# A decoder layer on one core: where the expert matmuls of the cross phase stand in the slots, and a gate of sixteen columns

## The chip, the cores and the metric

One core of one Trainium2 chip. The metric is the device time of one execution in microseconds, the median of three runs.

## What is computed

Eight sequences of 512 tokens and 512 features pass one decoder layer with a LayerNorm behind each of its three parts: a self-attention with a second, causal linear term; a cross-attention of 16 heads over a context of the same shape; and a feed-forward of two experts with a gate. Only the last part and the output projection of the second are touched. Cut to what matters:

```python
x = layernorm(x + xattn(ctx, ctx, x, Wv, Wk, Wq, Wo, bo))      # ends in  out @ Wo.T + bo
logits = x @ gate_w                                            # [4096, 512] @ [512, 8]
topk_w, topk_idx = top_k(softmax(logits), 2)
e0, e1 = silu(x @ w0 + b0), silu(x @ w1 + b1)                   # each [4096, 512] @ [512, 512]
out = e0 * topk_w[0] * (topk_idx[0] == 0) + e1 * topk_w[1] * (topk_idx[1] == 1)
x = layernorm(x + out)
```

Everything is float32 to the outside. Large products are made of a high and a low part of each operand (`F32R` tiles), as high times high, low times high and high times low: three matmuls for one.

## The kernel before, in words

The program has three phases, written out by hand for each engine: self-attention, the memory term with its projection, and the cross phase, which this change is about. It fills the time from about 861 us to the end.

**Slots.** The cross phase goes through 512 slots, `n` = 0 to 511. A slot is one key tile of one head: 16 slots make a group of four heads, 64 slots a batch (one sequence). In each slot PE makes two matmuls of 512 columns: the transposed scores (L1576), of which ACT takes the exponential into `cpt` (L1839), and the scores of a slot 22 later (L1547), of which DVE takes the row maximum (L1557). PE may be two slots ahead of either: the scores of slot n wait for the exponential of slot n-2, and L1547 of slot n for the maximum of slot n-2. In each group, at its slot 9 and at slot 4 of the next, PE multiplies two key tiles by the values (L1618), and at slot 4 of the next it adds up the exponentials (L1654), of which POOL has by then added three tiles into `cross_added` (L2094, at slots 7, 11 and 15 of each group). DVE takes the reciprocals of the sums at slots 5 to 8 (L1929).

**Work behind.** Beside batch B's slots run the output projection, LayerNorm, gate, experts and last LayerNorm of batch B-1, at slots given by tables at L1477 to L1503. A slot number over 63 lies in the next batch. Each engine works through its own program in slot order, and within a slot in the order of `cross_slot_tensor` and its siblings. The steps:

- `PROJECT`: output projection, tile k of 128 tokens times chunk c of 512 features, three matmuls for each pair (L1722 to L1724), with one matmul for the bias ahead of c = 0 (L1668). `ADD`, `FACTORS`, `APPLY`: residual and second LayerNorm (DVE, POOL, ACT).
- `TRANSPOSE`: four transposes on PE of a finished tile (L1702). One slot later ACT copies the high part, and at `LOW` DVE makes the low part (L2355). Tiles k = 0, 2 use bank 6, and 1, 3 bank 7.
- `GATE`: four slots of three matmuls each (L203 to L205 in `triple`), with 8 stationary columns. `LOGITS`: four transposes to tokens by experts (L1714). DVE and ACT then make the two weights of each token in bank 7.
- `EXPERT`: eight units (4 tiles, 2 experts), each of 12 matmuls of 512 columns (L1749), three slots a unit, four matmuls a slot, from slot 44 to 67. Units 0 and 1 have their bias from PE, the others from ACT, which writes it to the bank ahead (`cross_bias_written`, L1891 to L1894).
- For each unit then: tanh on ACT (L1870) one slot after its last matmul, silu on DVE (L1975) one slot later, the gate's weight on ACT (L1875) one later, and the add to the tile on POOL (L2064) one later. Tanh of unit u waits for POOL's add of unit u-2, since there are two `tanh` tiles.
- `STATS3`, `FACTORS3`, `APPLY3`, `STORE`: the third LayerNorm and the output of each tile.

The last batch has nothing to hide behind and is done in a tail, which keeps its order of work.

## Time and profile before

| | us |
|---|---|
| median of 3 runs | 1716.77 |
| lowest, highest | 1716.08, 1717.36 |
| the profiled execution | 1717.48 |
| its span, first to last instruction | 1714.9 |
| granted clock of PE, mean | 0.988 of full speed |
| cross phase, first exponential to the last one of slot 511 | 861.1 to 1653.2 |
| one batch of 64 slots, undisturbed | 101.85 |

The span is 2.6 us shorter than the execution's own time. Between 1000 and 1600 us the granted clock is 1.00. The batches there repeat to within a few hundredths of a microsecond, so that one of them stands for six. The rows below are of the batch whose slot 0 has its exponential at 1255.0 us, and of the start of the next one, whose slot 0 has it at 1356.9.

### The profile page before, as it was taken

Reading aid. Unit: us, or ns where it says so; the run is one execution under the profiler, and the core shown is the slowest. Engines: PE = TensorE matmul, PEld = TensorE weight load, DVE = VectorE, ACT = ScalarE, POOL = GpSimd, SP = SyncE. Lnnn points to the kernel's source line nnn. Section 1 sums busy time; section 2 is a strip of 40 time slices with the busy share of each in tenths; the row PEclk is TensorE's granted clock in tenths of the full one; section 3 lists DMA queues with packets and bytes.
Section 4 is the critical chain, followed back from the end, with each engine's and each line's share of the span. In section 5 each row is a group of like instructions: output and inputs, shape, how many; then the busy total and the mean of one; then the engine's idle time right before and its main releaser. Section 6 shows DMA issues by size and latency. Waiting matters only on the chain.

```text
span 1714.9 us, 30931 instructions
## 1 busy us (share of the span) xinstructions
PE 1643.5 (96%) x10596; PEld 1118.3 (65%) x10596; DVE 1254.9 (73%) x2790; ACT 1004.7 (59%) x2010; POOL 1169.0 (68%) x967
## 2 busy tenths in 40 slices
PE   8999999999999889999998999999999999999998
PEld 5777777777777468877853556575565656656566
DVE  6777777777777567777876677868777687777745
ACT  4666666666665543333355566676666766666664
POOL 3566665666656555654467787878798787978874
PEclk8999999999999899999999999999999999999999
DMA  7665656656665455667436434525434443533210
GB/s 217 161 168 158 171 159 164 165 162 163 165 156 154 146 183 173 189 190 215 154 110 162 126 103 118 136 63 155 111 107 115 108 138 80 160 100 106 63 50 25
DMA packets 173463, 237.80 MB, mean 139 GB/s; under 512 B 22774, under 2 KB 76278, under 8 KB 173308
## 3 DMA queue, kind: packets, MB, share of 16 engines
q1 hardware_dynamic: 173308, 235.84, 49.9%
q8 instruction: 85, 1.39, 0.3%
q14 instruction: 70, 0.57, 0.1%
HBM read 92.10 MB, written 41.94 MB: 78 GB/s over the span
## 4 chain that ended last, share of the span: by engine, by line
PE 77%; POOL 10%; DVE 4%; issue 3%; DMA 3%; ACT 2%; SPq 1%; POOLq 0%; DVEq 0%; ACTq 0%
PE bank L1749 9%; PE bank L203 7%; POOL cross_added L2094 7%; PE bank L204 7%; PE bank L205 7%; PE bank L349 6%; PE bank L1576 5%; PE bank L1618 5%; PE bank L1547 5%; PE bank L403 5%; PE bank L416 4%; PE bank L1654 2%; PE bank L980 1%; PE bank L374 1%; PE bank L1006 1%
## 5 line engine op out<-in xcount | busy, mean ns | idle before, releaser
L1557 DVE TENSOR_REDUCE cross_negmax<-bank 128x1 f32<-128x512 f32 x512 | 337.7, 673 | 99.8 <-PE bank L1547 96.7
L1839 ACT ACTIVATE cpt<-bank 128x512 f32<-128x512 f32 x512 | 297.2, 593 | 139.0 <-PE bank L1576 115.6
L494 ACT ACTIVATE pt<-bank 128x256 f32<-128x256 f32 (+3 forms) x512 | 222.2, 437 | 209.2 <-PE bank L349 193.5
L2094 POOL TENSOR_TENSOR cross_added<-cross_added,cpt 128x2048 f32<-128x2048 f32 x61 | 280.1, 4591 | 14.0 <-ACT cpt L1839 13.4
L607 DVE CUSTOM_DVE_ANT_0 bank<-bank,future 128x128 f32<-128x128 f32 (+3 forms) x512 | 240.1, 489 | 64.0 <-PE bank L403 63.9
L1576 PE MATMUL bank<-cqk 98*128 98x512 f32 x512 | 224.8, 439 | 10.7 <-ACT cpt L1839 7.3
L1547 PE MATMUL bank<-cqk 96*128 96x512 f32 x512 | 215.1, 424 | 13.9 <-DVE cross_negmax L1557 11.0
L678 POOL TENSOR_SCALAR_AFFINE_SELECT pt<-pt 128x512 f32<-128x512 f32 x128 | 81.6, 638 | 214.0 <-ACT pt L494 213.9
L2094 POOL TENSOR_TENSOR cross_added<-cpt,cpt 128x2048 f32<-128x2048 f32 x32 | 146.6, 4582 | 83.7 <-ACT cpt L1839 83.7
L349 PE MATMUL bank<-qk 98*128 98x256 f32 (+2 forms) x512 | 180.2, 355 | 6.7 <-ACT pt L494 4.5
L403 PE MATMUL bank<-qk 96*128 96x256 f32 (+2 forms) x512 | 167.9, 329 | 3.9 <-DVE self_negmax L607 2.3
L1929 DVE RECIPROCAL bank<-bank 128x128 f32<-128x128 f32 x128 | 121.8, 954 | 67.2 <-PE bank L1654 67.2
L203 PE MATMUL bank<-xt_hi,w_hi 128*128 128x512 f32 x384 | 158.2, 412 | 2.5 <-DVE w_lo L566 1.9
L1576 PEld LDWEIGHTS bank<-cqk 98*128 98x128 f32 x512 | 97.0, 189 | 93.6 <-issue 39.9
L204 PE MATMUL bank<-xt_hi,w_lo 128*128 128x512 f32 x384 | 154.1, 401 | 0.0
L205 PE MATMUL bank<-xt_lo,w_hi 128*128 128x512 f32 x384 | 152.3, 397 | 0.0
L349 PEld LDWEIGHTS bank<-qk 98*128 98x128 f32 x512 | 96.3, 189 | 82.2 <-ACT pt L494 40.7
L644 DVE RECIPROCAL bank<-bank 128x128 f32<-128x128 f32 x128 | 121.9, 958 | 33.8 <-PE bank L374 33.8
L1547 PEld LDWEIGHTS bank<-cqk 96*128 96x128 f32 x512 | 95.9, 189 | 61.2 <-DVE cross_negmax L1557 39.2
L1618 PE MATMUL bank<-cpt,cv 128*32 128x512 f32 x1024 | 124.2, 603 | 0.0
L694 POOL TENSOR_TENSOR self_added<-self_added,pt 128x1024 f32<-128x1024 f32 x64 | 118.0, 1843 | 5.4
L694 POOL TENSOR_TENSOR self_added<-pt,pt 128x1536 f32<-128x1536 f32 x32 | 111.3, 3479 | 2.7
(213 smaller groups left out, 3622.4 us busy)
## 6 DMA issues: line engine op xcount, KB each, us to landing
qk<-stage SPq DMA_DIRECT2D x384, 128.0 KB, 2.4
cqk<-cstage SPq DMA_DIRECT2D x384, 128.0 KB, 2.4
scratch_memory<-memory SPq DMA_DIRECT2D x64, 256.0 KB, 3.7
ma<-scratch_memory SPq DMA_DIRECT2D x32, 512.0 KB, 4.0
raw<-in_x_t SPq DMA_DIRECT2D x32, 256.0 KB, 2.8
v<-in_x SPq DMA_DIRECT2D x32, 256.0 KB, 3.2
scratch_y_ar<-y_ar SPq DMA_DIRECT2D x32, 256.0 KB, 2.2
my_ar<-scratch_y_ar SPq DMA_DIRECT2D x32, 256.0 KB, 4.6
```

The source lines that it names most:

```text
L203: pe.matmul(out, a[0], b[0], start=first, stop=False)
L204: pe.matmul(out, a[1], b[0], start=False, stop=False)
L205: return pe.matmul(out, a[0], b[1], start=False, stop=last)
L349: pe.matmul(bank[:, 0:SEQ - q0], kq[0:98, 1, j, first:first + P], kq[0:98, 0, j, q0:SEQ], start=True, stop=True).then_inc(s.pe_st, 1)
L403: pe.matmul(bank[:, 0:max(keys, 256)], kq[0:96, 0, j, tile_of(qt)], kq[0:96, 1, j, 0:max(keys, 256)], start=True, stop=True).then_inc(s.pe ...
L607: dve.tensor_tensor_reduce(out=scores, in0=scores, in1=sh.future[:, SEQ - P * (qt + 1):SEQ], scale=-1.0, scalar=-NEG, op0=ALU.add, op1=ALU ...
L694: pool.tensor_tensor(out, old, pt[:, :, 0:SEQ - first], ALU.add).then_inc(s.pool_add, 1)
L1547: pe.matmul(max_bank(sh, m)[:, :], kq[0:96, 0, jm, tile_of(qt)], kq[0:96, 1, jm, :], start=True, stop=True).then_inc(s.pe_mx, 1)
L1557: dve.reduce_max(s.negmax[gm % 2][:, col:col + 1], max_bank(sh, m)[:, :], AX, negate=True).then_inc(s.dve_max, 1)
L1576: pe.matmul(sh.bank[2 + n % 2][:, :], kq[0:98, 1, j, tile_of(kt)], kq[0:98, 0, j, :], start=True, stop=True).then_inc(s.pe_st, 1)
L1839: act.activation(s.pt[step % 3][:, j, :], sh.bank[2 + n % 2][:, :], ACT.Exp, scale=SCALE_CROSS).then_inc(s.act_exp, 1)
L2094: pool.tensor_tensor(s.added[:, :, :], old[:, :, :], s.pt[step % 3][:, :, :], ALU.add).then_inc(s.pool_add, 1)
```

## The change

The tables move, and some of what they need is rewritten:

- The expert units start at slots 30, 41, 47, 51, 54, 58, 61 and 64, and take 6, 6, 4, 3, 4, 3, 3 and 3 slots. In slots 30 to 35 and 41 to 46 there are two expert matmuls a slot, in 47 to 50 and 54 to 57 three, in the rest four. They end at slot 66. Tanh, silu, weight and add follow by tables of their own.
- Unit 0 waits for tile 0's low part alone, and unit 1 for nothing of the gate. Of the biases, PE makes those of units 0 and 2, and ACT the six others.
- The banks: unit 0, 1 and all odd ones in bank 6, units 2, 4 and 6 in bank 7. Transposes of tiles 1 to 3 share bank 7, so that those of tiles 2 and 3 wait for the low part of the tile just before (slots 30 and 33, on DVE). `TRANSPOSE` and `LOW` of tile 3 come one slot later.
- The gate's high and low parts stand side by side as 16 stationary columns: two matmuls a chunk for three. The sum of both halves is made where the logits are turned: four float32 matmuls by a 16 x 8 matrix of ones take the place of the four transposes. ACT copies 16 rows for 8. The low weights now also meet the low activations, a term that was left out before.
- The projection's first six pairs stand at slots 5 to 10 for 4 to 9. The third LayerNorm's steps come up to three slots earlier.

```diff
-PROJECT = {4: (0, 0), 5: (0, 1), 6: (0, 2), 7: (1, 0), 8: (1, 1), 9: (1, 2), 15: (0, 3), 16: (1, 3), 17: (2, 0),
+PROJECT = {5: (0, 0), 6: (0, 1), 7: (0, 2), 8: (1, 0), 9: (1, 1), 10: (1, 2), 15: (0, 3), 16: (1, 3), 17: (2, 0),
...
-LOW = (29, 30, 33, 35)
-GATE, LOGITS, EXPERT = 37, 42, 44
+LOW = (29, 30, 33, 36)
+GATE, LOGITS = 37, 42
...
-STATS3, FACTORS3, APPLY3, STORE = (58, 64, 68, 76), (59, 65, 69, 78), (66, 71, 73, 81), (67, 72, 74, 82)
+STATS3, FACTORS3, APPLY3, STORE = (55, 62, 67, 75), (56, 63, 68, 77), (63, 70, 72, 80), (64, 71, 73, 81)
+UNIT = (30, 41, 47, 51, 54, 58, 61, 64)
+UNIT_SLOTS = (6, 6, 4, 3, 4, 3, 3, 3)
+PREFILL = {1: 39, 3: 50, 4: 53, 5: 57, 6: 60, 7: 63}
+TANH = (36, 47, 51, 54, 58, 61, 64, 67)
+SILU = (37, 48, 52, 55, 59, 62, 65, 68)
+WEIGH = (46, 49, 53, 56, 60, 63, 66, 69)
+JOIN = (47, 50, 54, 57, 61, 64, 67, 70)
...
-                    pe.wait_ge(s.dve_u, UNITS * b - 1 + k)
+                    pe.wait_ge(s.dve_u, UNITS * b - k)
...
-            pe.wait_ge(s.dve_x2t, TILES * b + k - 1)
+            pe.wait_ge(s.dve_x2t, TILES * b + k)
...
-        done = triple(pe, sh.bank[6][0:EXPERTS, :], (cw.gate_hi[:, c, :], cw.gate_lo[:, c, :]),
-                      (s.x2t_hi[:, c, :], s.x2t_lo[:, c, :]), c == 0, c == GROUPS - 1)
+        parts = sh.bank[7][0:2 * EXPERTS, :]
+        pe.matmul(parts, cw.gate[:, c, :], s.x2t_hi[:, c, :], start=(c == 0), stop=False)
+        done = pe.matmul(parts, cw.gate[:, c, :], s.x2t_lo[:, c, :], start=False, stop=(c == GROUPS - 1))
...
-            done = pe.transpose(sh.bank[7][:, k * EXPERTS:(k + 1) * EXPERTS], s.x1t[0:EXPERTS, tile_of(k)],
-                                sh.ident[0:EXPERTS, 0:EXPERTS])
+            done = pe.matmul(sh.bank[7][:, k * EXPERTS:(k + 1) * EXPERTS], s.x1t[0:2 * EXPERTS, tile_of(k)],
+                             cw.gate_sum[:, :], start=True, stop=True)
...
+        if u == 0:
+            pe.wait_ge(s.dve_x2t, TILES * b + 1)
+        elif u == 2:
+            pe.wait_ge(s.dve_gate, GATE_OPS * (b + 1))
+        else:
+            pe.wait_ge(s.act_bias, bias_written(b, u))
...
+    piece, pieces = 2 * at + half, 2 * UNIT_SLOTS[u]
+    for part in range(3 * GROUPS * piece // pieces, 3 * GROUPS * (piece + 1) // pieces):
```

How the built programs stand, in three places. In the rows L1576 and L1547 before are L1595 and L1566 after; L1749 is L1770, L1702 is L1721, L2094 is L2116, L2064 is L2086.

PE, slots 32 to 34, before:

```order
L1576 MATMUL bank<-cqk_131 128x512
L1547 MATMUL bank<-cqk_132 128x512
L1632 MATMUL bank<-x1t,a 128x512
L1576 MATMUL bank<-cqk_131 128x512
L1702 MATMUL bank<-ident,x_183 128x128 x4
L1547 MATMUL bank<-cqk_132 128x512
L1576 MATMUL bank<-cqk_131 128x512
L1547 MATMUL bank<-cqk_132 128x512
```

and now:

```order
L1595 MATMUL bank<-cqk_131 128x512
L1770 MATMUL bank<-exp_hi,x2t_lo 128x512
L1566 MATMUL bank<-cqk_132 128x512
L1651 MATMUL bank<-x1t,a 128x512
L1770 MATMUL bank<-exp_lo,x2t_hi 128x512
L1595 MATMUL bank<-cqk_131 128x512
L1770 MATMUL bank<-exp_hi,x2t_hi 128x512
L1566 MATMUL bank<-cqk_132 128x512
L1770 MATMUL bank<-exp_hi,x2t_lo 128x512
L1595 MATMUL bank<-cqk_131 128x512
```

Two matmuls of unit 0 stand in each slot, one ahead of the scores for the maximum and one behind; before, these slots had none.

PE, slot 4 (the matmuls by the values and the sums of a batch's last group stand here), before:

```order
L1576 MATMUL bank<-cqk_132 128x512
L1668 MATMUL bank<-bias_rows,bias_pick 128x512
L1722 MATMUL bank<-wo_hi,cy_hi 128x512
L1723 MATMUL bank<-wo_lo,cy_hi 128x512
L1724 MATMUL bank<-wo_hi,cy_lo_137 128x512
L1547 MATMUL bank<-cqk_133 128x512
L1618 MATMUL bank<-cpt_176,cv_178 32x512 x4
L1618 MATMUL bank<-cpt_174,cv_178 32x512 x4
L1654 MATMUL bank<-cross_added,ones 32x512 x4
```

and now, with the start of slot 5:

```order
L1595 MATMUL bank<-cqk_132 128x512
L1566 MATMUL bank<-cqk_133 128x512
L1637 MATMUL bank<-cpt_176,cv_178 32x512 x4
L1637 MATMUL bank<-cpt_174,cv_178 32x512 x4
L1673 MATMUL bank<-cross_added,ones 32x512 x4
L1595 MATMUL bank<-cqk_132 128x512
L1687 MATMUL bank<-bias_rows,bias_pick 128x512
L1742 MATMUL bank<-wo_hi,cy_hi 128x512
L1743 MATMUL bank<-wo_lo,cy_hi 128x512
L1744 MATMUL bank<-wo_hi,cy_lo_137 128x512
```

The projection's bias and first three matmuls have gone to slot 5, and slot 4 has only its own two and the group's work.

POOL, behind its add of slot 55 to that of slot 63 and one further (a row of `x` is the add of a unit to its tile, four rows from L187 to L193 a LayerNorm's factors), before:

```order
L2064 TENSOR_TENSOR x_183<-x_183,tanh_161 128x512
L2064 TENSOR_TENSOR x_183<-x_183,tanh_162 128x512
L187 TENSOR_SCALAR ln_rstd<-ln_mv 128x1
L189 TENSOR_TENSOR ln_rstd<-ln_rstd,ln_power 128x1
L191 TENSOR_TENSOR ln_shift<-ln_mv,ln_rstd 128x1
L193 TENSOR_SCALAR ln_shift<-ln_shift 128x1
L2094 TENSOR_TENSOR cross_added<-cross_added,cpt_176 128x2048
L2064 TENSOR_TENSOR x_183<-x_183,tanh_161 128x512
L2046 TENSOR_TENSOR cstage<-keys,cstage 128x512
L2094 TENSOR_TENSOR cross_added<-cross_added,cpt_174 128x2048
L2064 TENSOR_TENSOR x_183<-x_183,tanh_162 128x512
```

and now:

```order
L187 TENSOR_SCALAR ln_rstd<-ln_mv 128x1
L189 TENSOR_TENSOR ln_rstd<-ln_rstd,ln_power 128x1
L191 TENSOR_TENSOR ln_shift<-ln_mv,ln_rstd 128x1
L193 TENSOR_SCALAR ln_shift<-ln_shift 128x1
L2086 TENSOR_TENSOR x_183<-x_183,tanh_162 128x512
L2116 TENSOR_TENSOR cross_added<-cross_added,cpt_176 128x2048
L2086 TENSOR_TENSOR x_183<-x_183,tanh_161 128x512
L2068 TENSOR_TENSOR cstage<-keys,cstage 128x512
L187 TENSOR_SCALAR ln_rstd<-ln_mv 128x1
L189 TENSOR_TENSOR ln_rstd<-ln_rstd,ln_power 128x1
L191 TENSOR_TENSOR ln_shift<-ln_mv,ln_rstd 128x1
L193 TENSOR_SCALAR ln_shift<-ln_shift 128x1
```

Here two adds to `x` stood ahead of the add of slot 59, and one stands there now; the factors of the next tile have come ahead of the add of slot 63.

## Rows read from the trace of the kernel before

**Rows 1.** The page: busy us (share of the span) and instructions of each engine.

```profile
PE 1643.5 (96%) x10596; PEld 1118.3 (65%) x10596; DVE 1254.9 (73%) x2790; ACT 1004.7 (59%) x2010; POOL 1169.0 (68%) x967
```

**Rows 2.** PE's waits, whole run: engine line <- waited for: us, times, longest.

```profile
PE bank L1547 <- DVE cross_negmax L1557: 11.0, 24, 0.8
PE bank L1654 <- POOL cross_added L2094: 9.7, 9, 1.5
```

**Rows 3.** Stretches A to D: length, busy us (instructions) of PE, PEld, DVE, ACT, POOL; clock; DMA.

```profile
1310.84:1340.93 30.09, 30.09 (x153) 18.91 (x154) 20.68 (x44) 17.84 (x34) 19.86 (x8) 1.00 0.48 117
1340.93:1366.75 25.82, 25.82 (x132) 17.52 (x130) 17.98 (x31) 18.96 (x37) 22.68 (x17) 1.00 0.27 69
1366.75:1389.64 22.89, 22.02 (x110) 14.03 (x107) 18.86 (x32) 13.40 (x24) 22.14 (x17) 1.00 0.52 157
1389.64:1412.69 23.05, 21.24 (x108) 11.57 (x109) 19.72 (x33) 17.00 (x32) 19.73 (x21) 1.00 0.48 122
```

**Rows 4.** Timeline of PE, slots 55 and 56: start, length, line, operation, [idle before it <- releaser].

```profile
1340.93 0.40 PE L1576 MATMUL bank<-cqk 98*128 98x512 f32 x1
...
1342.33 0.40 PE L1576 MATMUL bank<-cqk 98*128 98x512 f32 x1
```

**Rows 5.** Timeline of PE, slots 30 to 36.

```profile
1300.37 0.39 PE L1576 MATMUL bank<-cqk 98*128 98x512 f32 x1
...
1301.15 0.60 PE L1626 MATMUL bank<-ident,x_group 128*128 128x128 f32 x4
1301.51 0.48 PE L1576 MATMUL bank<-cqk 98*128 98x512 f32 x1
...
1303.54 1.02 PE L1632 MATMUL bank<-x1t,a 128*128 128x512 f32 x2
1303.99 0.80 PE L1576 MATMUL bank<-cqk 98*128 98x512 f32 x1
1304.63 0.60 PE L1702 MATMUL bank<-ident,x 128*128 128x128 f32 x4
...
1307.87 1.92 PE L1618 MATMUL bank<-cpt,cv 128*32 128x512 f32 x16
1310.84 1.06 PE L1654 MATMUL bank<-cross_added,ones 128*32 128x512 f32 x8 [1.05 <-POOL cross_added L2094]
```

**Rows 6.** Timeline of POOL, slot 55 to slot 15 of the next batch.

```profile
1343.26 4.61 POOL L2094 TENSOR_TENSOR cross_added<-cpt,cpt 128x2048 f32<-128x2048 f32 x1 [7.08 <-ACT cpt L1839]
...
1363.68 1.29 POOL L2064 TENSOR_TENSOR x<-x,tanh 128x512 f32<-128x512 f32 x1
...
1384.91 4.58 POOL L2094 TENSOR_TENSOR cross_added<-cross_added,cpt 128x2048 f32<-128x2048 f32 x1
```

**Rows 7.** Timeline of ACT, slots 55 and 4.

```profile
1341.45 0.60 ACT L1891 ACTIVATE bank<-bias 128x512 f32<-128x512 f32 x1 [0.88 <-DVE tanh L1975]
...
1342.60 0.58 ACT L1839 ACTIVATE cpt<-bank 128x512 f32<-128x512 f32 x1
...
1365.06 0.60 ACT L1870 ACTIVATE tanh<-bank 128x512 f32<-128x512 f32 x1 [2.43 <-POOL x L2064]
1365.55 0.59 ACT L1839 ACTIVATE cpt<-bank 128x512 f32<-128x512 f32 x1
```

**Rows 8.** Timeline of PE at the logits, slot 42.

```profile
1319.58 0.41 PE L1714 MATMUL bank<-ident,x1t 8*128 8x8 f32 x4
1319.92 0.50 PE L1547 MATMUL bank<-cqk 96*128 96x512 f32 x1
```

**Rows 9.** DVE, 1153 to 1560 us, by line: busy us, mean ns | idle before.

```profile
L1929 DVE RECIPROCAL bank<-bank 128x128 f32<-128x128 f32 x64 | 61.2, 956 | 30.2 <-PE bank L1654 30.2
```

**Rows 10.** Timeline of PE, slot 14.

```profile
1276.81 0.50 PE L1547 MATMUL bank<-cqk 96*128 96x512 f32 x1 [0.81 <-DVE cross_negmax L1557]
```

**Rows 11.** Timeline of DVE, slots 29 and 30.

```profile
1300.68 0.67 DVE L2355 TENSOR_TENSOR x2t_lo<-bank,x2t_hi 128x512 fp32r<-128x512 f32 x1
1301.28 0.67 DVE L1557 TENSOR_REDUCE cross_negmax<-bank 128x1 f32<-128x512 f32 x1
```

More of the change, by code:

```diff
@@ L1742, in cross_expert @@
             pe.wait_ge(s.act_bias, bias_written(b, u))
-        if u < 2:
+        if b == 0 and u < 2:
+            pe.wait_ge(s.pool_exp_lo, 2 * GROUPS - 1 + u)
+        if u not in PREFILL:
             cross_bias(pe, cw, bank, 1 + i)
-    for part in range(4 * third + 2 * half, 4 * third + 2 * half + 2):
+    piece, pieces = 2 * at + half, 2 * UNIT_SLOTS[u]
+    for part in range(3 * GROUPS * piece // pieces, 3 * GROUPS * (piece + 1) // pieces):
         c, which = divmod(part, 3)
@@ L1869, in cross_batch_scalar @@
             act.wait_ge(s.pool_x2, UNITS * b + u - 1)
[L1870 to L1871 removed]
+        act.activation(s.tanh[u % 2][:, :], unit_bank(sh, u)[:, :], ACT.Tanh, scale=0.5).then_inc(s.act_tanh, 1)
+    if slot in WEIGH:
+        u = WEIGH.index(slot)
         k, i = divmod(u, 2)
```

86 lines of the change are left out of this document (44 added, 42 removed).

## The prediction

> **What bounds the kernel now.** I began with the page. PE is busy for 1643.5 us, 96% of the span [rows 1], and no other engine is near it. But a busy PE is no full PE: in slot 55 six matmuls of 512 columns follow each other, and slot 56 begins 1.40 us after it, 0.233 us for each, though a row says 0.40 us long [rows 4]. I take 0.233 us as the price of one. A light slot, with the two score matmuls alone, lasts longer than its 0.47 us: from slot 30's first matmul to slot 31's it is 1.14 us, with 0.36 us of transposes in it [rows 5]. Such gaps count as busy. So the list of PE's waits, with only 11.0 us for DVE's maxima and 9.7 us for POOL's sums [rows 2], is a lower bound.
>
> Then the windows. I cut a batch of 101.85 us at four marks [rows 3]: A, from the sums of slot 36 (L1654) to the scores of slot 55; B, from there to the scores of slot 5 of the next batch; C, to the sums of slot 20; D, to the sums of slot 36 again. A and B are full of PE work. C ends on PE and POOL at once: POOL's add of slot 15 starts at 1384.91 and takes 4.58 us, and the sums follow at 1389.64 [rows 3, 6]. D ends on POOL: PE stood 1.05 us idle before the sums at 1310.84 [rows 5]. The granted clock is 1.00, 2.4 GHz, in all four, so no term of the clock enters.
>
> The rule of the Trainium skill, Perfetto Trace Analysis, section Identifying the Most-Contended Engine, is that PE's matmul busy share is no measure of how full PE is. The trace agrees: busy 0.40 us rows at a pace of 0.233 us. By the busy share taken at its word, D had 1.81 us to fill (23.05 less 21.24), and unit 0 would cost D 1.2 us instead of the 0.7 us below.
>
> **The change, part by part.** Each sum is for one batch.
>
> *A, 30.09 us.* Before: 12 gate matmuls, 44 of experts (slots 44 to 54) and two biases, 58. After: 8 of the gate, 39 of experts and one bias, 48. Ten fewer are -2.3 us. The logits' four float32 matmuls for four transposes: the old ones held PE 0.34 us [rows 8]; the nearest float32 matmul (L1632, 512 columns) comes as two rows and, with the lateness of the matmul behind it, takes some 0.9 us [rows 5], but has 64 times the columns. If every matmul now counts twice at the old pace, that is +0.25 us; ends -0.1 and +0.9. Then DVE: in slots 37 to 40 it has a reciprocal and a maximum, 0.96 us long by its row [rows 9], and 0.6 us from start to start for an operation of 512 columns [rows 11]: with the overlap of one's end and the next one's start some 1.46 us a slot. PE now needs 4 x 0.233 = 0.93 us for such a slot, before 1.17 us. DVE has silu of unit 0 in slot 37 as well. So its maximum of slot 39 ends 3 x 1.46 + 0.6 = 5.0 us behind the sums, and PE asks for it in slot 41, 4 x 0.93 us and two matmuls behind them, at 4.3 us. I take +0.5 us; ends 0 and +0.9 us (a whole slot of PE). A: -2.3 + 0.25 + 0.5 = -1.55 us.
>
> *B, 25.82 us.* Experts had 52 matmuls from slot 55 on and have 45; a bias and three projection matmuls leave slot 4. Eleven fewer are -2.6 us on PE. But tanh of unit 7 moves from slot 68 to 67, slot 3, and still waits for POOL's add of unit 5. That wait was 2.43 us already, till 1365.06 [rows 7], when POOL was done with its add at 1363.68 [rows 6]. It now holds the exponential of slot 3, for which the scores of slot 5 wait. From POOL's add of slot 55 to the end of unit 5's add stand the same operations as before, 21.7 us (1343.26 to 1364.97). POOL's start, though, comes earlier: the exponential of slot 55 stood behind a bias that had waited 0.88 us for silu, and a weight [rows 7], and ran 1.67 us behind its scores of 1340.93 [rows 4]. In the new tables ACT has neither in slot 55. So 1.1 us from scores to POOL's start (0.5 to the exponential, 0.58 its length), 21.7 us on POOL, 0.5 us to the exponential behind tanh (1365.06 to 1365.55), 0.6 us till it is done: 24.0 us. PE alone would need 23.2 us. B is 24.0 us, -1.8 us; ends -2.6 (PE alone) and -0.6 us (POOL starts 2.33 us behind the scores, as before).
>
> *C, 22.89 us.* The four matmuls from slot 4 stand here now: +0.93 us. In slot 14 PE waited 0.81 us for DVE [rows 10]; a PE that comes later waits less. I take +0.7 us; ends 0 and +0.93 us. POOL has one add to a tile fewer between slot 55 and slot 15, 1.28 us, and so allows the earlier sums.
>
> *D, 23.05 us.* Thirteen new matmuls, 3.0 us, in slots 30 to 35, where PE had gaps. What PE does from slot 30's scores to the sums is then 27 matmuls of 512 columns (6.3 us), three times four transposes (0.36 us each), the query (0.45 us), the values (1.9 us), and about 0.7 us by which matmuls behind float32 ones are late (0.64 us instead of 0.233 behind the query) [rows 5]: 10.45 us. Ahead of it, unit 0 waits for tile 0's low part, which DVE began at 1300.68 and ended at 1301.35 [rows 11], 0.75 us behind PE's scores of slot 30. The sums would start at 1311.57, not 1310.84: +0.7 us; ends 0 and +1.2 us. Transposes of tiles 2 and 3 wait for DVE one slot nearer; PE comes to them later than before, so I cost that at nothing. If that cover is gone, see the third rival.
>
> *Beside other work.* ACT's one more half bias a batch, 0.60 us at most by the row of a whole one [rows 7], lies beside PE in B, where ACT is busy 18.96 of 25.82 us [rows 3]; uncovered it costs its length. DVE's small sum matrix is one operation of the whole run. Output stores are issued up to three slots earlier and so only leave SP's queue sooner.
>
> *The sum.* A, C and D come with seven batches, B with six; behind the last batch only the seven expert matmuls go, -1.6 us: 7 x (-1.55 + 0.7 + 0.7) + 6 x (-1.8) - 1.6 = -1.05 - 10.8 - 1.6 = -13.5 us. The profiled execution took 1717.48 us, its span 1714.9 us; the 2.6 us around it don't change: 1704.0 us. It lies 0.7 us over the median, which gives **1703.3 us**. With B at its better end and C and D at nothing it is 4.8 and 9.8 us less, 1689; with B and D at their worse ends 7.2 and 3.5 us more, 1714.
>
> The Trainium skill, TensorE: Matmul & The Clock Gate, section Back-to-back issue gap, has about 131 ns for a matmul of 512 columns in a stream with weight loads. The trace shows 233 ns [rows 4], and the sum goes by it; by the page's figure the ten matmuls of A would be worth 1.3 us and the eleven of B 1.4 us, which is an estimate from that page.
>
> **The rivals.**
>
> *1. The gaps take up everything.* A gives 2.2, B 2.6, C and D cost nothing: 7 x -2.2 + 6 x -2.6 - 1.6 = -32.6 us, **1684 us**. For it: D has more gaps than its waits show, and DVE is idle in A for 9 of 30 us [rows 3]. Against it: POOL is busy 22.68 of 25.82 us in B, and the sums of D wait for it. 20%.
>
> *2. POOL and ACT hold the batch where it is.* The exponential of slot 55 stays late, B gives only 0.6 us, DVE in A takes its upper end and the logits theirs (-0.5 us), C and D cost 0.93 and 0.75 us: 7 x 1.2 - 6 x 0.6 - 1.6 = +3.2 us; with the logits at 0.25 us it is -1.4 us. **About 1717 us**, no change. For it: POOL's busy share in B and C. Against it: ACT's queue at slot 55 is empty by the tables. 12%.
>
> *3. PE loses its lead over DVE, and it gets slower.* PE now asks at slots 31, 34 and 37 for what DVE does one slot before, where it asked with a slot more of room. If DVE is a full slot late there, PE waits each time for one maximum and one low part, 1.2 us, and then DVE waits for PE's next matmul: D costs 3 x 1.2 = 3.6 us more, 7 x 3.6 = 25 us, **1729 us**. It is slower than before from 13.5 / 21 = 0.65 us a place on, about one DVE operation [rows 11]. Against it: the low part of tile 0 costs PE 0.75 us, but behind it PE has 0.7 us more work a slot than it had. 8%.
>
> That the edits do not do what they say is hardly a rival: matmuls are gone from the program.
>
> **How the numbers follow.** My forecast has 60%, with its own range 1692 to 1712. The range of all is 1688 to 1713: it leaves out the third rival, the better part of the second and half of the first. A measurement of this kernel tells some 0.2%, 3.4 us, from no change, so faster means under 1713.3 us. The first rival and nearly all of the forecast are faster; the second is mostly the same, and the third slower: 0.83, 0.09, 0.08.
>
> **What would show it.** In the new profile the exponentials of slot 0 should be 99.9 us apart. In the windows A should be near 28.5, B 24.0, C 23.6, D 23.8 us. ACT's exponential of slot 55 should run within 0.6 us of its scores, and PE's scores of slot 5 should wait behind tanh of unit 7 (L1891 of the new kernel). The sums of slot 36 should no longer wait for POOL. I am wrong if PE waits for DVE's low parts in slots 31 to 37 for more than 0.5 us each, if PE's sums of slot 20 or 52 wait for POOL, or if a batch takes less than 98 us.

## The result, and the profile after

The changed kernel took **1727.0 us** (median of 6 runs, 1720.6 to 1730.2) against 1716.8 us for the kernel before: a ratio of 1.0051, 95% interval [1.0031, 1.0071]. Two more measurements below gave 1.0028 [1.0011, 1.0045] and 1.0029 [1.0009, 1.0049]. It is **slower**, by 0.3 to 0.5%; I had forecast 1703.3 us, and "slower" had 0.08. The profiled execution took 1720.6 us, its span 1718.9 us.

The engines' busy time, the page of the changed kernel, answering to [rows 1]:

```profile
PE 1640.3 (95%) x10596; PEld 1121.3 (65%) x10596; DVE 1256.8 (73%) x2791; ACT 1003.5 (58%) x2017; POOL 1168.3 (68%) x967
```

PE is busy 3.2 us less, and the span is 4 us longer, so waits or gaps came. (The number of PE's instructions is the same by chance: four gate matmuls a batch went, and the logits' four float32 matmuls are eight rows where the transposes were four.) PE's waits, over the whole run, answering to [rows 2] (engine, line, releaser: us in total, times, longest):

```profile
PE bank L1566 <- DVE cross_negmax L1576: 13.4, 30, 0.7
PE bank L1595 <- ACT cpt L1860: 9.4, 16, 3.6
...
PE bank L1687 <- DVE x2t_lo L2382: 4.5, 7, 0.7
...
PE bank L1566 <- ACT cpt L1860: 3.7, 8, 0.7
PE bank L1673 <- POOL cross_added L2116: 3.3, 3, 1.8
...
PE bank L1687 <- DVE tanh L1997: 2.6, 6, 0.4
```

POOL's share fell from 9.7 to 3.3 us, as forecast. The other lines shown are DVE or ACT. The stretches of the batch that answers to [rows 3], in the order A, B and then C, D of one batch, C and D lying ahead of A in time (length, busy us of PE, PEld, DVE, ACT, POOL, granted clock, DMA):

```profile
1314.37:1343.76 29.39, 28.96 (x151) 17.86 (x144) 20.85 (x44) 18.96 (x38) 20.35 (x9) 1.00 0.48 117
1343.76:1368.38 24.62, 23.68 (x122) 15.45 (x120) 16.78 (x30) 16.31 (x34) 22.41 (x17) 1.00 0.28 76
1266.11:1290.52 24.41, 23.25 (x110) 14.72 (x114) 19.78 (x34) 14.30 (x26) 21.94 (x18) 1.00 0.55 154
1290.52:1314.37 23.85, 22.66 (x126) 14.18 (x122) 20.00 (x33) 17.47 (x32) 19.77 (x19) 1.00 0.43 110
```

| us | before | forecast | after |
|---|---|---|---|
| A, sums of slot 36 to scores of slot 55 | 30.09 | 28.5 | 29.39 |
| B, to the scores of slot 5 | 25.82 | 24.0 | 24.62 |
| C, to the sums of slot 20 | 22.89 | 23.6 | 24.41 |
| D, to the sums of slot 36 | 23.05 | 23.8 | 23.85 |
| batch | 101.85 | 99.9 | 102.27 |

D is right. C has 0.8 us too much, A 0.9 us, B 0.6 us. The granted clock is 1.00 in all four, as before. To find the places I took, for every slot, the time from its first score matmul to that of the next slot, as the mean of five batches. Three places that stand out are shown in rows. First the end of the old batch, slots 3 to 5:

```profile
1264.97 0.60 ACT L1891 ACTIVATE tanh<-bank 128x512 f32<-128x512 f32 x1 [3.43 <-POOL x L2086]
...
1266.11 0.50 PE L1595 MATMUL bank<-cqk 98*128 98x512 f32 x1 [0.37 <-ACT cpt L1860]
...
1267.05 0.51 PE L1687 MATMUL bank<-bias_rows,bias_pick 128*128 128x512 f32 x1 [0.44 <-DVE tanh L1997]
```

ACT's tanh of unit 7 waits 3.43 us for POOL (forecast: POOL's chain), behind it the exponential of slot 3, behind that the scores of slot 5 (0.37 us). So POOL's chain sets the end of B, as forecast; it is longer than forecast, and that is taken up below. Then the bias for the projection waits 0.44 us for DVE's silu of unit 7, which the text had not named. Second, slots 37 to 41, where DVE does a reciprocal and a maximum a slot (in slot 37 silu of unit 0 as well), and PE waits (the row with the wait names ACT, whose exponential ended at 1320.46; by the code this matmul waits for DVE's maximum of slot 39, which ended at 1320.43; experiment 8 decides for DVE):

```profile
1315.48 0.97 DVE L1951 RECIPROCAL bank<-bank 128x128 f32<-128x128 f32 x1 [1.57 <-PE bank L1673]
1316.35 0.67 DVE L1997 SCALAR_TENSOR_TENSOR tanh<-tanh,bank 128x512 f32<-128x512 f32 x1
...
1318.94 0.95 DVE L1951 RECIPROCAL bank<-bank 128x128 f32<-128x128 f32 x1
...
1319.80 0.63 DVE L1576 TENSOR_REDUCE cross_negmax<-bank 128x1 f32<-128x512 f32 x1
...
1320.35 0.95 DVE L1951 RECIPROCAL bank<-bank 128x128 f32<-128x128 f32 x1
...
1320.49 0.50 PE L1566 MATMUL bank<-cqk 96*128 96x512 f32 x1 [0.43 <-ACT cpt L1860]
...
1323.11 0.39 PE L1595 MATMUL bank<-cqk 98*128 98x512 f32 x1
...
1323.43 1.05 PE L1734 MATMUL bank<-gate_sum_parts,x1t 16*128 16x8 f32 x8
...
1324.42 0.50 PE L1770 MATMUL bank<-exp_lo,x2t_hi 128*128 128x512 f32 x1
```

The last three rows are the logits: four float32 matmuls of eight columns, shown as eight rows, hold PE from 1323.43 to 1324.42, 0.99 us, where the four transposes took 0.34 us [rows 8]. Third, slot 57: DVE has silu of unit 3 and the statistics of the last norm for tile 0 ahead of a maximum, and PE waits for it:

```profile
1345.19 0.67 DVE L1997 SCALAR_TENSOR_TENSOR tanh<-tanh,bank 128x512 f32<-128x512 f32 x1
...
1345.78 0.68 DVE L178 BATCH_NORM_STATS2 ln_stats<-x 128x6 f32<-128x512 f32 x1
...
1346.60 0.66 DVE L1576 TENSOR_REDUCE cross_negmax<-bank 128x1 f32<-128x512 f32 x1
...
1347.31 0.50 PE L1566 MATMUL bank<-cqk 96*128 96x512 f32 x1 [0.59 <-DVE cross_negmax L1576]
```

### The profile page after: what moved, and what is told of

Its sections match the earlier page's. It is cut to its first block, busy times and chain, and to the rows that moved or that the text cites. A ratio compares the mean times of both kernels' runs of the same rounds, so it can differ in the third digit from the quotient of the medians.

```text
span 1718.9 us, 30940 instructions
## 1 busy us (share of the span) xinstructions
PE 1640.3 (95%) x10596; PEld 1121.3 (65%) x10596; DVE 1256.8 (73%) x2791; ACT 1003.5 (58%) x2017; POOL 1168.3 (68%) x967
## 4 chain that ended last, share of the span: by engine, by line
PE 70%; DVE 9%; POOL 8%; issue 6%; DMA 3%; ACT 2%; SPq 1%; POOLq 0%; DVEq 0%; ACTq 0%
PE bank L203 7%; PE bank L204 6%; PE bank L205 6%; PE bank L349 6%; PE bank L1770 5%; POOL cross_added L2116 5%; PE bank L403 5%; PE bank L1637 5%; PE bank L1566 4%; PE bank L416 4%; PE bank L1595 4%; DVE cross_negmax L1576 3%; DVE bank L1951 2%; PE bank L1006 2%; PE bank L980 1%
## 5 line engine op out<-in xcount | busy, mean ns | idle before, releaser
L1576 DVE TENSOR_REDUCE cross_negmax<-bank 128x1 f32<-128x512 f32 x512 | 339.3, 673 | 111.2 <-PE bank L1566 108.0
L2116 POOL TENSOR_TENSOR cross_added<-cross_added,cpt 128x2048 f32<-128x2048 f32 x61 | 280.6, 4599 | 35.0 <-ACT cpt L1860 34.6
L1566 PE MATMUL bank<-cqk 96*128 96x512 f32 x512 | 213.0, 419 | 20.4 <-DVE cross_negmax L1576 13.4
L1595 PE MATMUL bank<-cqk 98*128 98x512 f32 x512 | 219.1, 428 | 12.0 <-ACT cpt L1860 9.4
L2116 POOL TENSOR_TENSOR cross_added<-cpt,cpt 128x2048 f32<-128x2048 f32 x32 | 146.4, 4575 | 55.4 <-ACT cpt L1860 55.4
L1595 PEld LDWEIGHTS bank<-cqk 98*128 98x128 f32 x512 | 97.2, 190 | 80.8 <-issue 32.1
L1566 PEld LDWEIGHTS bank<-cqk 96*128 96x128 f32 x512 | 96.3, 190 | 71.8 <-DVE cross_negmax L1576 49.4
```

What stands on the lines that cost most here:

```text
L1566: pe.matmul(max_bank(sh, m)[:, :], kq[0:96, 0, jm, tile_of(qt)], kq[0:96, 1, jm, :], start=True, stop=True).then_inc(s.pe_mx, 1)
L1576: dve.reduce_max(s.negmax[gm % 2][:, col:col + 1], max_bank(sh, m)[:, :], AX, negate=True).then_inc(s.dve_max, 1)
L1595: pe.matmul(sh.bank[2 + n % 2][:, :], kq[0:98, 1, j, tile_of(kt)], kq[0:98, 0, j, :], start=True, stop=True).then_inc(s.pe_st, 1)
L2116: pool.tensor_tensor(s.added[:, :, :], old[:, :, :], s.pt[step % 3][:, :, :], ALU.add).then_inc(s.pool_add, 1)
```

## The experiments

Ratios are to the kernel before, measured beside each. **Theory 1**: PE's new waits for DVE and ACT, where their work now stands one slot nearer, and the dearer logits eat what the matmuls save. **Theory 2**: POOL's chain of adds holds the batch, whatever PE saves. **Theory 3**: the granted clock is lower in some executions. "The spread kernels" are those with the new tables. **Theory 4** came with experiment 10: a transfer lost its room.

**1. The changed kernel again.** No edit.

> The changed kernel itself once more. Its stretches were C 24.40, D 23.83, A 29.39, B 24.62 us against 22.88, 23.07, 30.08, 25.82 of the kernel before, so a batch is 102.3 us instead of 101.85. Theory 1 (slot by slot waits of PE on DVE and ACT, and dearer logits, eat the saving): the same stretches within 0.1 us, median 1721 to 1730 us. Theory 3 (part of the 0.5% is a lower granted clock that only some executions show): executions at 1721 us have a mean granted clock of 0.988, those at 1730 us of 0.98 or less, and the median falls on one of the two groups.

1722.6 us, ratio 1.0028 [1.0011, 1.0045]. The stretches are A 29.36, B 24.67, C 24.40, D 23.80 us to within 0.05 us in batches 2 to 6. Executions ran from 1717.0 us (mean granted clock 0.989) to 1730.3 us (0.979), without two groups. Most of that clock is lost ahead of the cross phase, where the kernels don't differ: between 550 and 650 us it is 0.91 in the profile of before, 0.90 in this one and 0.83 in a third one of the changed kernel at 1732.0 us. So theory 3 explains the scatter of all kernels, not the 0.3% that all three measurements show. The first measurement's 0.5% may be it in part: four of its six executions had a mean clock of 0.984 or less.

**2. The spread without the gate.**

```diff
-        pe.matmul(parts, cw.gate[:, c, :], s.x2t_hi[:, c, :], start=(c == 0), stop=False)
-        done = pe.matmul(parts, cw.gate[:, c, :], s.x2t_lo[:, c, :], start=False, stop=(c == GROUPS - 1))
+        done = triple(pe, sh.bank[7][0:EXPERTS, :], (cw.gate[:, c, 0:EXPERTS], cw.gate[:, c, EXPERTS:]),
+                      (s.x2t_hi[:, c, :], s.x2t_lo[:, c, :]), c == 0, c == GROUPS - 1)
...
-            done = pe.matmul(sh.bank[7][:, k * EXPERTS:(k + 1) * EXPERTS], s.x1t[0:2 * EXPERTS, tile_of(k)],
-                             cw.gate_sum[:, :], start=True, stop=True)
+            done = pe.transpose(sh.bank[7][:, k * EXPERTS:(k + 1) * EXPERTS], s.x1t[0:EXPERTS, tile_of(k)],
+                                sh.ident[0:EXPERTS, 0:EXPERTS])
```

> The changed kernel with the old gate: three matmuls a slot in slots 37 to 40 and four small transposes for the logits; the spread tables stay. Theory 1 (the float32 logits cost 0.65 us, and in slots 37 to 41 DVE is late so that PE's fewer matmuls gain nothing in full): four gate matmuls +0.93, logits -0.65, wait of slot 41 -0.4: -0.1 us a batch in A, 1726 us, the same as the changed kernel within 2 us. Theory 2 (POOL holds the batch): no difference either, but the sums of slots 20 and 52 wait for POOL. If logits and DVE cost nothing: +0.93 us a batch, 1733 us.

**1716.2 us**, ratio 0.9987 [0.9971, 1.0004], 6 us less than the changed kernel. The time of slots 37 to 41 together is **7.77 us with and without the four matmuls**; they are worth nothing there. A is 28.76 us, -0.61 us, all of it in slot 42 (2.12 to 1.47 us), the logits. B, C and D are as in the changed kernel:

```profile
1316.77:1345.53 28.76, 28.76 (x151) 17.60 (x144) 20.85 (x44) 19.05 (x38) 20.43 (x9) 1.00 0.49 119
```

**3. The gate alone**, in the tables of before (the same edit the other way).

> The kernel before with the new gate alone (sixteen columns, float32 logits), tables as before. Theory 1: gate -0.93 us, logits +0.65 us, DVE's lateness in slot 41 up to +0.4 us: -0.28 to +0.1 us a batch in A, 1715 to 1717.5 us. As I predicted the logits (+0.25 us) and DVE: -0.2 to -0.7 us a batch, 1712 to 1715 us. Theory 2: no difference, 1717 us, for another reason: then A itself would be shorter and B longer by the same.

1720.9 us, ratio 1.0015 [1.0000, 1.0030]. Slots 37 to 41 together are 7.08 us against 7.31 us: -0.24 us for four matmuls of 0.93 us, since slot 41 grows by 0.71 us. Slot 42 grows by 0.64 us. A is 0.44 us longer, B, C, D unchanged:

```profile
1313.10:1343.63 30.53, 29.95 (x154) 19.24 (x154) 20.69 (x44) 17.68 (x34) 19.85 (x8) 1.00 0.47 115
1343.63:1369.49 25.86, 25.86 (x132) 17.53 (x130) 17.95 (x31) 19.04 (x37) 22.75 (x17) 1.00 0.26 69
```

So the gate part of the change is a loss in either surrounding, 7 times 0.44 us here and 7 times 0.61 us in experiment 2, and both sides of it were mis-sized: -0.24 us where I had -0.43 (four matmuls less DVE's 0.5), +0.64 where I had +0.25.

**4. The same gate, logits by transposes**, the two halves added by DVE, in the tables of before. On top of the edit of experiment 3:

```diff
+            done = pe.transpose(sh.bank[7][:, 128 + k * 2 * EXPERTS:128 + (k + 1) * 2 * EXPERTS],
+                                s.x1t[0:2 * EXPERTS, tile_of(k)], sh.ident[0:2 * EXPERTS, 0:2 * EXPERTS])
...
+        dve.tensor_copy(s.lg[:, :, :], both[:, :, EXPERTS:]).then_inc(s.dve_half, 1)
+        dve.wait_ge(s.dve_half, 2 * b + 1)
+        dve.tensor_tensor(gate_scratch(sh.bank[7], 0), both[:, :, 0:EXPERTS], s.lg[:, :, :],
+                          ALU.add).then_inc(s.dve_half, 1)
```

> The kernel before with the new gate, but logits by four small transposes of sixteen rows and two operations more on DVE to add the parts. gate_alone had slots 37 to 41 0.24 us shorter and slot 42 0.64 us longer. Theory 1: here slot 42 is as before (1.11 us), slots 37 to 41 keep their -0.24 us, and DVE's two operations cost up to 0.4 us in slots 43 to 45: A between 29.85 and 30.25 us against 30.09, 1716 to 1719 us. If transposes of sixteen rows cost PE more than those of eight, slot 42 is over 1.2 us.

1718.6 us, ratio 0.9999 [0.9981, 1.0017]. Slot 42 is back at 1.11 us, A is 30.22 us: slots 37 to 41 keep -0.24 us and slot 45 pays +0.38 us to DVE. Sixteen rows cost PE no more than eight.

**5. The same in the changed kernel.**

> The changed kernel, but its logits come by four small transposes of sixteen rows (0.34 us before), and DVE adds high and low part with two operations of 32 columns more in slot 43. Theory 1 (the four float32 matmuls cost PE 0.65 us more than transposes, in slot 42): slot 42 goes from 2.12 to 1.5 us, A from 29.36 to 28.75 us, 0.6 us a batch, 1718.5 us against the changed kernel's 1722.6. If the 0.65 us were DVE's lateness and not PE's price, slot 42 stays at 2.1 us and the time at 1722.6 us.

1722.0 us, ratio 1.0027 [1.0010, 1.0043]. Slot 42 falls to 1.48 us as expected, but slot 45 grows from 1.08 to 1.52 us: A 29.19 us, -0.17 and not -0.6 us. PE came earlier, and DVE had two operations more.

**6. The projection back at slot 4.** Tile 0 goes through bank 7, which unit 6 leaves early.

```diff
-PROJECT = {5: (0, 0), 6: (0, 1), 7: (0, 2), 8: (1, 0), 9: (1, 1), 10: (1, 2), 15: (0, 3), 16: (1, 3), 17: (2, 0),
+PROJECT = {4: (0, 0), 5: (0, 1), 6: (0, 2), 7: (1, 0), 8: (1, 1), 9: (1, 2), 15: (0, 3), 16: (1, 3), 17: (2, 0),
-LOW = (29, 30, 33, 36)
+LOW = (28, 29, 33, 36)
...
-        bank = sh.bank[6 + k % 2]
+        bank = sh.bank[7 - k % 2]
...
-    return sh.bank[6 if k == 0 else 7]
+    return sh.bank[6 if k == 1 else 7]
...
-            pe.wait_ge(s.dve_x2t, TILES * b + 1)
+            pe.wait_ge(s.dve_x2t, TILES * b + 2)
```

> The changed kernel with the next batch's projection back in slots 4 to 9 (its first tile in bank 7, which unit 6 leaves early), and the low part of tile 0 in slot 28, tile 1 in slot 29. Theory 1 (the four matmuls moved to slot 10 were paid in full, +0.93 us in C, and slot 5 got two waits, 0.37 us of its scores for ACT and 0.44 us of its bias for DVE's silu of unit 7): C back to 23.1 us (-1.3), B +0.5 us: -0.8 us a batch, 1721 us by medians (5 to 6 us less than the changed kernel). Theory 2 (POOL's and ACT's chain sets the start of slot 5): B keeps its length, the wait only moves to slot 4 or 5, 1727 us, no gain.

1722.1 us, ratio 1.0020 [1.0007, 1.0033]: no gain in the time. Yet C is 22.80 us in five of seven batches (-1.6 us), slot 5 is back at 1.27 us and slot 10 at 0.58 us, and B has only 0.45 us more. So theory 1 holds for C. It was given back twice: D is 24.4 us (+0.6 us; unit 0 in slot 30 now has to wait for the low part of tile 1, slot 30 lasts 3.31 us instead of 2.51) and in one batch 26.0 us, and two batches had C at 24.3 and 24.4 us, which is the matter of experiments 10 and 11.

**7. Unit 1 in slots 44 to 46.**

```diff
-UNIT = (30, 41, 47, 51, 54, 58, 61, 64)
-UNIT_SLOTS = (6, 6, 4, 3, 4, 3, 3, 3)
-PREFILL = {1: 39, 3: 50, 4: 53, 5: 57, 6: 60, 7: 63}
-SILU = (37, 48, 52, 55, 59, 62, 65, 68)
+UNIT = (30, 44, 47, 51, 54, 58, 61, 64)
+UNIT_SLOTS = (6, 3, 4, 3, 4, 3, 3, 3)
+PREFILL = {1: 43, 3: 50, 4: 53, 5: 57, 6: 60, 7: 63}
+SILU = (42, 48, 52, 55, 59, 62, 65, 68)
```

> The changed kernel with unit 1 in slots 44 to 46 (four matmuls a slot) instead of 41 to 46, and DVE's silu of unit 0 in slot 42 instead of 37 (ACT's bias of unit 1 in slot 43). Theory 1 (slots 37 to 41 go at DVE's pace, behind reciprocals, maxima and silu, so PE's fewer gate matmuls gain nothing): six matmuls leave slots 41 to 43 (-1.4 us) for 44 to 46 (+1.4 us), but slot 41 falls from 3.69 to about 3.0 us or less because silu no longer stands ahead of its maximum: A 28.8 us, -0.5 us a batch, 1719 us. If PE were the bound in slots 37 to 43, A stays at 29.36 us and the time at 1722.6 us.

1720.8 us, ratio 1.0020 [1.0003, 1.0037]; A 29.20 us, a third of the gain expected. Slots 37 to 41 fall from 7.77 to 7.08 us, the same 7.08 us as in experiment 3, where PE and DVE have the same work there. That is five times the 1.41 us from one reciprocal to the next in the rows above; and the 0.69 us more of the changed kernel are about silu of unit 0 (0.67 us by its row). The edit moved silu and PE's matmuls of unit 1 together, so this is argued from the lengths and not shown.

**8. The reciprocals cut short**, 16 of 128 columns each. It leaves seven eighths of the sums as they are, so its output is not the layer's.

```diff
-        sums = sh.bank[5][:, tile_of(at - 5)]
+        sums = sh.bank[5][:, P * (at - 5):P * (at - 5) + 16]
```

> The changed kernel, but each of DVE's reciprocals takes 16 columns instead of 128, so most of the sums stay unreciprocated (left out: seven eighths of the normalisation). Theory 1 (DVE is the bound in slots 37 to 41 and behind slot 55): slots 37 to 41 from 7.77 us to PE's own 6.9 us or less, A 28.4 us, slot 57 from 4.06 to 3.3 us, B 23.9 us; slots 4 to 9 and 20 to 25 may gain too: 2 us a batch or more, 1708 us or less. Theory 2 (POOL's chain holds the batch): A and slot 57 may gain, but the sums of slots 20, 36, 52 wait for POOL by as much: batch 102 us, 1722 us.

1705.8 us, ratio 0.9929 [0.9903, 0.9954], with the same matmuls as the changed kernel. Slots 37 to 41 take 6.82 us, A 28.42 us, D 22.86 us, slot 57 3.22 us; no sums waited for POOL more than before (2.4 us in all, 3.3 in the changed kernel). DVE is the bound in these places, and for A and D theory 2 falls.

For B it does not. Slot 57 gained 0.84 us, but B only 0.43 (24.62 to 24.19): slot 4 grew from 3.71 to 4.12 us, and PE's scores of slot 5 waited there, behind the exponential behind tanh of unit 7, behind POOL. POOL's add of slot 59 and its add of unit 5, in the changed kernel (the batch of A and B above):

```profile
1344.87 4.59 POOL L2116 TENSOR_TENSOR cross_added<-cpt,cpt 128x2048 f32<-128x2048 f32 x1 [1.90 <-ACT cpt L1860]
...
1352.67 4.61 POOL L2116 TENSOR_TENSOR cross_added<-cross_added,cpt 128x2048 f32<-128x2048 f32 x1 [0.43 <-ACT cpt L1860]
...
1365.87 1.27 POOL L2086 TENSOR_TENSOR x<-x,tanh 128x512 f32<-128x512 f32 x1
```

and with the short reciprocals, POOL and then PE's scores of slot 5:

```profile
1336.96 4.60 POOL L2116 TENSOR_TENSOR cross_added<-cpt,cpt 128x2048 f32<-128x2048 f32 x1 [1.90 <-ACT cpt L1860]
...
1357.53 1.28 POOL L2086 TENSOR_TENSOR x<-x,tanh 128x512 f32<-128x512 f32 x1
...
1360.04 0.49 PE L1595 MATMUL bank<-cqk 98*128 98x512 f32 x1 [0.77 <-ACT cpt L1860]
```

From POOL's add of slot 55 to the end of its add of unit 5 it takes 22.27 us there and 21.85 us here: the 0.43 us for which POOL waited in slot 59, because slot 57 was late, are gone, and the rest of the chain stands.

**9. Statistics of tiles 0 and 1 back behind slot 57.**

```diff
-STATS3, FACTORS3, APPLY3, STORE = (55, 62, 67, 75), (56, 63, 68, 77), (63, 70, 72, 80), (64, 71, 73, 81)
+STATS3, FACTORS3, APPLY3, STORE = (58, 63, 67, 75), (59, 64, 68, 77), (63, 70, 72, 80), (64, 71, 73, 81)
```

> The changed kernel with the statistics of tile 0 in slot 58 instead of 55, those of tile 1 in slot 63 instead of 62. Theory 1 (slot 57 lasts 4.06 instead of 3.45 us because statistics and silu of unit 3 both stand in slot 55 ahead of DVE's reciprocals' last and the maxima): slot 57 back to about 3.5 us, B 24.1 us, 1719 us. Theory 2 (B is held by POOL's chain of adds to slot 3, so a gain in slot 57 is given back as a longer wait of slot 5's scores): B stays at 24.65 us and slot 5 grows from 2.21 to 2.7 us, 1722.6 us.

**1713.9 us**, ratio 0.9978 [0.9961, 0.9995], 9 us under the changed kernel's 1722.6 of experiment 1. Slot 57 lasts 3.27 us, B 23.40 us (-1.25), C 24.06 us (-0.35; slot 5 1.86 instead of 2.21 us). Slot 4 is shorter too, 3.28 instead of 3.71 us, which neither theory had. POOL's factors moved with the statistics, those of tile 1 from ahead of the add of slot 63 to behind the add of unit 5, and experiment 8 takes the two apart: with slot 57 short and the factors where the change put them, PE waited 0.77 us for that chain and B was 24.19 us. Here the chain takes 20.71 us, and the scores of slot 5 wait for nothing:

```profile
1361.83 0.50 PE L1595 MATMUL bank<-cqk 98*128 98x512 f32 x1
```

So of the gain in B some 0.4 us are DVE's statistics alone, and the other 0.8 need POOL's factors out of the way as well. That split is read from the two traces; no run moved the factors alone.

**10. Tile 3 one slot later.** The expectation speaks of output stores, and so misreads the table: the edit moves tile 3's statistics from slot 75 to 76, its factors from 77 to 78, its application from 80 to 81 and its store from 81 to 82.

```diff
+STATS3, FACTORS3, APPLY3, STORE = (55, 62, 67, 76), (56, 63, 68, 78), (63, 70, 72, 81), (64, 71, 73, 82)
```

> The changed kernel with the output stores issued in slots 76, 78, 81 and 82 as before, not 75, 77, 80, 81. In single batches the scores of slot 16 waited up to 1.5 us for the small transfer of the shift rows, issued in slot 12. If the store of slot 75 (slot 11), ahead of it on SP, is the cause: no such batch, C 24.40 us in all seven, some 1 us less in all, 1721.5 us against 1722.6. If not: single batches with C over 25 us stay, and the time is 1722.6 us. The kernel before had such waits too (2.3 us in all), so I lean to the second.

1718.6 us, ratio 1.0014 [0.9995, 1.0033]. C is 24.23 us in all batches from the second on (-0.17 us), and no batch has a long C. The long batches went, as the expectation's first outcome had it, but not for its reason, since no store ahead of that transfer moved. Slot 75 is slot 11 of the next batch, and DVE makes the low part of the shift rows in slot 12. With the statistics ahead of it the small transfer of these rows is issued 2.54 us before the scores of slot 16 would use them, without them 3.33 us.

**11. Tile 3's statistics, and its factors, one slot earlier in the kernel before.**

```diff
-STATS3, FACTORS3, APPLY3, STORE = (58, 64, 68, 76), (59, 65, 69, 78), (66, 71, 73, 81), (67, 72, 74, 82)
+STATS3, FACTORS3, APPLY3, STORE = (58, 64, 68, 75), (59, 65, 69, 77), (66, 71, 73, 81), (67, 72, 74, 82)
```

> The kernel before with DVE's statistics of tile 3 in slot 75 instead of 76 and POOL's factors in slot 77 instead of 78, nothing else. Theory 4 (the statistics stand ahead of the low part of the shift rows in slot 76, so the transfer is issued 0.8 us later; it lands in 1.8 us mostly and in up to 4.0 us now and then, and the scores of slot 80 wait for it): the first of its two issues 2.5 us ahead of these scores instead of 3.3 us, slot 13 1.39 instead of 0.59 us and slot 14 1.14 instead of 1.94 us, one or two of seven batches with C or D's first slots 1 to 1.7 us longer: 1719 to 1720 us against 1717.5. Rival (the DVE wait of slot 14 only changes its slot, transfers scatter as before): C 22.89 us in all, 1717.5 us.

1719.8 us, ratio 1.0015 [0.9996, 1.0035], too small to tell from no change by the time. The trace tells it: two of its batches have C at 23.93 and 24.30 us instead of 22.89. One of them, engine SP's issue and PE's scores of slot 15 and 16:

```profile
1371.79 0.27 DVE L1944 TENSOR_TENSOR cross_shift<-bank,cross_shift 16x128 fp32r<-16x128 f32 x1
...
1372.12 1.20 SPq L800 DMA_DIRECT2D cqk<-cross_shift  x2
...
1373.41 0.48 PE L1576 MATMUL bank<-cqk 98*128 98x512 f32 x1
...
1375.86 0.50 PE L1576 MATMUL bank<-cqk 98*128 98x512 f32 x1 [1.05 <-DMA cqk<-cross_shift]
```

In the kernel before, same place of its batch:

```profile
1376.94 0.27 DVE L1944 TENSOR_TENSOR cross_shift<-bank,cross_shift 16x128 fp32r<-16x128 f32 x1
...
1377.13 0.67 DVE L178 BATCH_NORM_STATS2 ln_stats<-x 128x6 f32<-128x512 f32 x1
...
1377.27 1.20 SPq L800 DMA_DIRECT2D cqk<-cross_shift  x2
...
1379.35 0.48 PE L1576 MATMUL bank<-cqk 98*128 98x512 f32 x1
...
1380.60 0.40 PE L1576 MATMUL bank<-cqk 98*128 98x512 f32 x1
```

The transfer (from issue to landing 1.8 us at the least and in the median, 4.0 at the most) is there after 2.54 us in most batches and not in some. Over all profiles here, batches 2 to 7: with 2.54 us of room (ten profiles, three of them of the changed kernel) 14 of 60 batches were longer by it, 0.8 to 1.7 us each; with 3.33 us (eight profiles) none of 48.

**12. All statistics moved back, all else of the change kept.**

```diff
+STATS3, FACTORS3, APPLY3, STORE = (58, 63, 67, 76), (59, 64, 68, 78), (63, 70, 72, 81), (64, 71, 73, 82)
```

> The changed kernel with all statistics of the last norm where PE does not wait for DVE: tile 0 in slot 58, 1 in 63, 2 in 67, 3 in 76 (factors one slot behind, the last in 78, application and store of tile 3 in 81 and 82). Everything that the change does for PE stays. stats58 had B 23.40 us, C 24.05 us with single batches of 24.9 to 25.6 us; the run with tile 3 moved back had C 0.17 us shorter and no such batch. Theory 1 with 4: C 23.9, D 23.8, A 29.4, B 23.4 us: 100.5 us a batch, 1711 us, faster than before by 0.4%. Theory 2 (POOL holds the batch): 1716 us or more, with sums waiting for POOL.

**1711.1 us**, ratio 0.9957 [0.9937, 0.9977]; and, measured beside it, the changed kernel a third time:

> The changed kernel once more, beside the others of this call. Theories 1 and 4: stretches as before (C 24.40, D 23.82, A 29.37, B 24.65 us), one or two batches of seven with C over 25 us, 1721 to 1725 us; against after_stats_back 10 to 12 us slower.

1724.6 us, ratio 1.0029 [1.0009, 1.0049]. Eight entries of a table, none of them PE's, are 13 us and turn the sign. Stretches A to D:

```profile
1310.80:1340.19 29.39, 28.96 (x151) 17.85 (x144) 20.86 (x44) 18.96 (x38) 20.33 (x9) 1.00 0.48 117
1340.19:1363.59 23.40, 23.40 (x122) 15.45 (x120) 17.26 (x31) 16.65 (x35) 21.24 (x16) 1.00 0.28 76
1363.59:1387.48 23.89, 22.91 (x115) 14.90 (x115) 19.42 (x33) 13.98 (x26) 23.03 (x18) 1.00 0.57 161
1387.48:1411.30 23.82, 22.63 (x126) 14.19 (x122) 20.00 (x33) 17.40 (x32) 19.84 (x20) 1.00 0.45 112
```

**13. Together.** Experiment 6, 7 and 12, unit 0 in slots 31 to 35, and the logits of experiment 5 (best2), then with the old gate instead (best3). In the expectation of best2 "output stores back" again stands for tile 3 of the last norm.

```diff
+UNIT = (31, 44, 47, 51, 54, 58, 61, 64)
+UNIT_SLOTS = (5, 3, 4, 3, 4, 3, 3, 3)
```

> All of it together: projection from slot 4 with tile 0 in bank 7, unit 0 in slots 31 to 35, unit 1 in 44 to 46, silu of unit 0 in slot 42, statistics of tile 0 in slot 58, output stores back in slots 76, 78, 81, 82, logits by transposes. Theory 1: C 22.85, D 23.6, A 28.0, B 24.5 us, 99.0 us a batch: 1700 us. Theory 2 (POOL and ACT hold the batch near 101.8 us): 1717 us, with waits of PE's sums of slots 20 and 52 for POOL.

> The combination of the run before (best2: 1704.5 us, batch of 99.78 us), but with the old gate: three matmuls a slot in slots 37 to 40 and the logits by four transposes of eight rows; DVE then has no adding of high and low parts. Theory 1 (slots 37 to 41 go at DVE's pace, 1.41 us for a reciprocal and a maximum, so four matmuls fewer are worth 0.24 us there, and less than nothing once DVE has more to do in slots 43 to 45): slots 37 to 41 +0.24 us, slot 45 from 2.00 to 1.55 us, so -0.2 us a batch: 1703 us, not slower than best2. If the merged gate is worth its four matmuls: +0.93 us a batch, 1711 us.

best2 1704.5 us, ratio 0.9929 [0.9910, 0.9947]; **best3 1703.2 us, ratio 0.9909 [0.9882, 0.9937]**, faster than either kernel. A is 29.02 us with the new gate and 28.80 with the old. Stretches A to D of best3:

```profile
1298.12:1326.92 28.80, 28.80 (x151) 17.72 (x144) 20.88 (x44) 19.06 (x38) 20.45 (x9) 1.00 0.49 118
1326.92:1351.24 24.32, 24.32 (x125) 16.20 (x124) 18.17 (x32) 17.46 (x36) 22.13 (x16) 1.00 0.30 81
1351.24:1373.85 22.61, 21.80 (x110) 14.19 (x110) 18.52 (x32) 13.27 (x24) 21.77 (x18) 1.00 0.55 156
1373.85:1397.66 23.81, 22.64 (x126) 14.19 (x122) 20.00 (x33) 17.37 (x32) 20.14 (x20) 1.00 0.47 119
```

**14. Weight pieces earlier.** D of the first batch was 25.1 to 28.0 us long in the spread kernels so far, 24.4 in the kernel before.

```diff
-SPLIT_EXPERT = tuple(range(29, 29 + 10 * 2 * GROUPS, 10))
+SPLIT_EXPERT = tuple(range(29, 29 + 8 * 2 * GROUPS, 8))
```

> best3 (1703.2 us) with the eight pieces of the experts' weights split every eighth slot from 29 on (the last in slot 85) instead of every tenth (slot 99), so that ACT and POOL are done with them before slot 94, where unit 0 of the first batch starts. If the late pieces make D of the first batch 1.6 us or more longer than the others' 23.8 us: D 23.8 to 24.2 us there and 1701.5 us. If not (other work or the granted clock): D stays at 25.5 us or more, 1703 us.

1702.2 us, ratio 0.9912 [0.9892, 0.9932], the same as best3 in time; D of the first batch is 23.81 us in its one trace, against 25.47 in that of best3, which speaks for the pieces. In some traces the clock fell there as well, after gaps of PE in slots 24 to 28: in the second profile of the changed kernel 0.69 between 995 and 1000 us, that is part of it at the lower of the two levels (1.2 GHz):

```profile
990.00:995.00 5.00, 3.55 (x14) 2.14 (x15) 4.96 (x11) 3.40 (x7) 4.45 (x7) 0.96 0.02 3
995.00:1000.00 5.00, 5.00 (x20) 3.93 (x18) 2.16 (x4) 2.39 (x4) 5.00 (x3) 0.69 0.03 9
```

In the first profile of the changed kernel it stayed at 1.00 there. Why in one and not in the other I did not settle.

## Why the prediction was wrong, by its steps

- **What bounds the kernel: right as far as it went.** PE's pace of 0.233 us held for every matmul that moved where PE is the bound: slots 49, 50 and 54 to 56 lose 0.23 us each. By the busy share D would have cost 1.2 us, by the pace 0.7; it was 0.76. That bears out the rule of the Trainium skill, Perfetto Trace Analysis, section Identifying the Most-Contended Engine. The 131 ns of the Trainium skill, TensorE: Matmul & The Clock Gate, section Back-to-back issue gap, do not fit these rows; 0.233 us do. But the pace tells a saving only where PE is the bound of that very slot.
- **D, +0.7: right, and by its mechanism** (+0.80 in the rows, +0.76 in the mean). From the scores of slot 30 to the sums I had 11.20 us; the rows have 11.24 (1303.13 to 1314.37):

```profile
1303.13 0.40 PE L1595 MATMUL bank<-cqk 98*128 98x512 f32 x1
...
1304.17 0.50 PE L1687 MATMUL bank<-bias_rows,bias_pick 128*128 128x512 f32 x1 [0.63 <-DVE x2t_lo L2382]
```

  The wait for tile 0's low part is there each batch (4.5 us in 7), and the sums of slot 36 no longer wait for POOL. The third rival's places, slots 31, 34 and 37, cost nothing.
- **A, -1.55, measured -0.70: the term of the gate failed**, that is, DVE's +0.5. I let PE's four matmuls count in full and took 0.5 us off for DVE. But slots 37 to 41 go at DVE's 1.41 us for a reciprocal and a maximum (experiments 2, 3, 7, 8). So DVE took 1.0 us and not 0.5 (-0.70 is -2.3 + 0.64 + 1.0): the four matmuls are worth 0.24 us, and nothing once silu of unit 0 stands there too. I had the pace and the place, and asked only whether one maximum was late, not what all five slots last. The maximum of slot 39 ended 6.06 us behind the sums (1314.37 to 1320.43) and not 5.0: I had named silu of unit 0 and left its length out, and the first reciprocal began only 1.11 us behind the sums. The logits were +0.64, inside my ends of -0.1 and +0.9, not +0.25.
- **B, -1.8, measured -1.20: the statistics were costed at nothing, and POOL's chain was misread.** That POOL's chain bounds B was right, and so was its start, 1.11 us behind the scores of slot 55. But it took 22.27 us and not 21.7. I named output stores among the moved steps and passed over the statistics of tile 0, which went from slot 58 to 55, ahead of the maximum that PE waits for in slot 57; POOL's add of slot 59 then waited 0.43 us for its exponential. Nor are they "the same operations as before": one add to a tile fewer (1.28 us), and the four operations of tile 1's factors more (1.42 us, 1359.88 to 1361.30). With DVE out of the way B is 24.19 us (experiment 8), near my 24.0. With statistics and factors behind, it is 23.40 us, -2.42 us, by my "better end, PE alone" of -2.6.
- **C, +0.7, measured +1.52: no cover.** The four matmuls cost their full 0.93 us. The DVE wait of slot 14 that was to absorb part did not: with slot 10 longer DVE too started later (it was idle 2.09 us for PE's maximum of slot 10), and with the statistics of tile 3 one slot earlier the wait only moved to slot 13. The rest, some 0.6 us, is slot 5: its bias behind silu (not named). The wait of its scores behind ACT (named) ends before the slot begins and is part of B.
- **What no term had:** single batches that wait for the shift rows (experiments 10, 11), 0 to 4 us a run, and the first batch's D, 25.4 to 27.8 us in the three profiles against 24.4.
- **Behind the last batch** it was -2.6 us (from the last exponential to the end 61.8 to 59.2 us), not -1.6.
- **The sum by what was measured:** 7 x (-0.69 + 0.76 + 1.52) + 6 x (-1.20) - 2.6 = +1.3 us. In the last batch A was 0.15 us longer and not 0.69 shorter (0.8 us more), and the two irregular items come on top. From slot 5 of the second batch, where the changed work begins, to the end the three profiles are 3.3, 5.4 and 8.1 us longer than that of before; the medians of the three measurements lie 5 to 10 us over before. With the statistics back: 7 x (-0.69 + 0.76 + 1.01) + 6 x (-2.42) - 2.6 = -9.5 us; measured -8.2 us.
- **The rivals.** The outcome is near the third in kind, PE losing its lead over DVE, but at slots 5, 41 and 57, not at 31, 34, 37, and at half its price. It had 8%. By the sum the second came nearer, with +3.2 us: A -0.5, B -0.6, C +0.93, D +0.75 against -0.70, -1.20, +1.52, +0.76. It had 12%; it was right that POOL bounds B, and in A and C it was DVE. I had tested the tables of PE for such places and not those of DVE.

## What to carry over

When a table of slots changes, cost every entry in it, on every engine, those of small operations on an engine that is 73% busy above all: list for each slot what that engine now has ahead of the operation that the busiest engine waits for. The same goes for the order on the engine that bounds a stretch: four small operations of POOL, 1.42 us, stood ahead of the one that others waited for or behind it, and that was worth some 0.8 us a batch. A saving on the bound engine counts only up to the next engine's pace in that same slot; ask of each slot what it would last if the saved work were free. And look how much room a transfer has before its user: it is either enough for its worst landing or it costs some batches.

## What was not expected of the hardware

- A float32 matmul of 16 rows by 128 with eight columns is two rows of 0.251 us; four of them hold PE 0.99 us, four transposes 0.34 us, of sixteen rows as of eight. So such a matmul costs what one of 512 columns of the large products costs, 0.233 us.
- DVE's reciprocal of 128 x 128 takes 0.96 us, longer than any of its operations on 128 x 512 in the cross phase (0.68 us), and with the maxima four in a row set the pace of slots 37 to 41.
- An 8 KB transfer between two on-chip tiles lands in 1.8 us in the median and in up to 4.0 us. What makes a single one late no run here shows.
- Between 550 and 650 us the mean granted clock was 0.83 in some executions and 0.91 in others of the same code, and the first exponential of the cross phase came at 859.8 to 868.2 us in the three profiles of the changed kernel.
